# Second layers of two expert stages: two experts to one product of 512 columns

## The reference, cut to what matters

```python
mW1 = W1 + jnp.einsum('be,efh->bfh', g, TW1)
mW2 = W2 + jnp.einsum('be,ehf->bhf', g, TW2)
u = jax.nn.gelu(jnp.einsum('bsh,bfh->bsf', x, mW1) + mb1[:, None, :])
out = jnp.einsum('bsf,bhf->bsh', u, mW2) + mb2[:, None, :]
```

```python
for ei in range(e):
    h = jax.nn.gelu(xf @ W1[ei] + b1[ei], approximate=False)
    y = h @ W2[ei] + b2[ei]
    out = out + y * (gf * mask)[:, None]
```

## Time and profile before

| | |
|---|---|
| median of 3 executions | 468.69 us (468.10 to 469.07) |
| span of the profiled execution | 467.3 us |
| TensorE busy | 449.3 us, 96% |
| VectorE, ScalarE, GpSimd busy | 256.2, 240.2, 123.5 us |
| second layers of stage 1 (L1850, L1830) | about 286.6 to 314.3 us |
| second layers of stage 2 | about 440.0 to 464.5 us |

### The profile page before, as it was taken

How to read it: one execution, slowest core, us unless ns; L and a number is a source line. 1 busy time by engine, 2 the same in 40 slices (tenths; PEclk the granted TensorE clock), 3 DMA queues, 4 the chain that set the end, 5 groups by cost and what they waited for, 6 DMA issues and landing times.

```text
span 467.3 us, 8504 instructions
## 1 busy us (share of the span) xinstructions
PE 449.3 (96%) x3500; PEld 385.6 (83%) x3500; DVE 256.2 (55%) x455; ACT 240.2 (51%) x439; POOL 123.5 (26%) x113
## 2 busy tenths in 40 slices
PE   8999999999999999999987999999999999999997
PEld 7887989989897989899966677998666779778797
DVE  2656223245426232232045788985567765469996
ACT  2577334264445343242113777762788764347872
POOL 1110000002000500000021277966920000019795
PEclk9999999999999999999999999999999999999999
DMA  8925400005200020000039999998000039264000
GB/s 281 412 96 194 180 2 1 1 0 183 89 0 1 13 90 1 1 1 1 1 121 426 362 294 337 420 389 361 2 1 1 2 119 418 96 269 181 0 1 13
DMA packets 13191, 62.65 MB, mean 134 GB/s; under 512 B 1365, under 2 KB 3813, under 8 KB 7392
## 3 DMA queue, kind: packets, MB, share of 16 engines
q1 hardware_dynamic: 11072, 54.31, 30.8%
q0 software_dynamic: 2080, 7.80, 4.7%
HBM read 61.97 MB, written 0.13 MB: 133 GB/s over the span
## 4 chain that ended last, share of the span: by engine, by line
PE 76%; DVE 6%; ACT 5%; DMA 5%; POOL 3%; issue 3%; SPq 0%; DVEq 0%; ACTq 0%; POOLq 0%
PE W L1590 20%; PE W L1546 15%; PE W L1749 7%; PE W L1830 4%; DMA ctxmem<-units_dram 4%; PE W L1884 4%; PE W L1929 3%; PE W L1563 3%; POOL w_lo L552 3%; PE W L1947 2%; PE W L1612 2%; PE W L1469 2%; DMA fixed<-units_dram 1%; PE W L1871 1%; PE W L1498 1%
## 5 line engine op out<-in xcount | busy, mean ns | idle before, releaser
L1590 PE MATMUL W<-probs_turned_hi,ctx_split_hi 128*128 128x256 f32 x256 | 72.8, 285 | 2.6 <-issue 2.5
L1590 PE MATMUL W<-probs_turned_hi,ctx_split_lo 128*128 128x256 f32 x256 | 72.4, 283 | 0.0
L1590 PE MATMUL W<-probs_turned_lo,ctx_split_hi 128*128 128x256 f32 x256 | 72.4, 283 | 0.0
L1024 DVE TENSOR_TENSOR probs_turned_lo<-W,probs_turned_hi 128x512 fp32r<-128x512 f32 x32 | 20.6, 686 | 64.9 <-ACT probs_turned_hi L693 64.9
L1590 PEld LDWEIGHTS W<-probs_turned_hi,ctx_split_hi 128*128 128x128 f32 x256 | 49.1, 192 | 3.8 <-issue 3.3
L561 POOL TENSOR_TENSOR small<-small,const 128x1 f32<-128x1 f32 (+2 forms) x10 | 7.0, 697 | 163.4 <-DVE small L1097 75.3
L1590 PEld LDWEIGHTS W<-probs_turned_lo,ctx_split_hi 128*128 128x128 f32 x256 | 49.1, 192 | 0.2
L1590 PEld LDWEIGHTS W<-probs_turned_hi,ctx_split_lo 128*128 128x128 f32 x256 | 49.1, 192 | 0.0
L712 ACT ACTIVATE pbuf<-W,small 128x1024 f32<-128x1024 f32 x16 | 17.9, 1116 | 59.6 <-DVE small L1044 59.6
L552 POOL TENSOR_TENSOR w_lo<-arena,w_hi 128x320 fp32r<-128x320 f32 x30 | 41.3, 1390 | 26.1 <-ACT w_hi L634 25.6
L552 POOL TENSOR_TENSOR w_lo<-ctxmem,w_hi 128x320 fp32r<-128x320 f32 (+1 forms) x30 | 46.3, 1568 | 5.1 <-ACT w_hi L634 4.6
(11 more groups left out here) (403 smaller groups left out, 907.6 us busy)
## 6 DMA issues: line engine op xcount, KB each, us to landing
arena<-units_dram SPq DMA_DIRECT2D x22, 1024.0 KB, 11.5
ctxmem<-units_dram SPq DMA_DIRECT2D x16, 1024.0 KB, 15.2
fixed<-units_dram SPq DMA_DIRECT2D x6, 1024.0 KB, 6.1
pbuf<-ctx_dram POOLq DMA_DIRECT2D x4, 512.0 KB, 6.3
ctxmem<-ctxT_dram SPq DMA_DIRECT2D x8, 256.0 KB, 11.8
ctxmem<-ctx_dram SPq DMA_DIRECT2D x2, 1024.0 KB, 14.6
scr<-ctx_dram POOLq DMA_DIRECT2D x3, 512.0 KB, 4.2
vecs<-vectors_dram POOLq DMA_DIRECT2D x1, 1040.0 KB, 7.6
```

The source lines that it names most:

```text
L1024: dve.tensor_tensor(PT[1][at], bank(4 + c).rearrange("p (t m) -> p t m", t=4), f32(PT[0][at]), ALU.subtract).then_inc(ev("pl_sb"), 1)
L1590: mm = pe.matmul(ps, CXN[a][:, t, c * P:(c + 1) * P], PT[z][:, t, :], start=(t == 0 and n == 0), stop=(t == KEYT - 1 and n == 2))
```

## The change

Two experts `2m` and `2m + 1` form a pair. A half of a pair holds 2 tiles of both experts instead of 4 tiles of one, laid side by side: the splitting engines read from both units and write the parts with the experts' 256 columns next to each other, so that one product has 512 columns. The third half of a pair is still counted under the second unit, but each half reads both units. For this, `ctxmem` and `arena` become one tensor `memory`, in which both units of a pair are reached with one stride (`memory_of`, `flipped`). There are 24 products of 512 columns for a pair, where there were 48 of 256. `y_ps` counts one sum for a pair, and VectorE adds two experts after it, one behind the other (`add_pair`). The base matrix of stage 1 stays as it was (`base_of_layer2`); the first sum of stage 2 is now that of the pair `m2e0`, `m2e1` (`first_pair_of_layer2`). A unit's place is given free when the pair's last half has been split.

The core of the diff:

```diff
@@ plan_places @@
-            need += lo_done(half_of(before, 1))
+            need += lo_done(half_of(partner(before)[1] if paired(before) else before, 1))
...
-        def half_in(p):
-
-            return unit(SPLIT[p // 2])[:, (p % 2) * HALF:(p % 2 + 1) * HALF]
+        def half_in(p, lo=0, hi=HALF):
+
+            u = SPLIT[p // 2]
+            if paired(u):
+                t = 2 * (p - half_of(partner(u)[0], 0))
+                a, z = sorted(memory_of(v) for v in partner(u))
+                return memory[:, :].rearrange("p (u t c) -> p t u c", u=8 + NA, t=FT)[:, t:t + 2, a:z + 1:z - a, lo // 4:hi // 4]
+            return unit(u)[:, (p % 2) * HALF + lo:(p % 2) * HALF + hi]
...
+        def landed(p):
+
+            u = SPLIT[p // 2]
+            return [(ev(f"place{PLACE[v]}"), LANDED[v]) for v in (partner(u) if paired(u) else (u,))]
...
@@ keep_w_hi @@
-                    act.wait_ge(ev(f"place{PLACE[u]}"), LANDED[u])
+                    for place, count in landed(p):
+                        act.wait_ge(place, count)
...
+            def add_pair(m, n, weight):
+
+                dve.wait_ge(ev("y_ps"), OUTPUTS * n + m + 2)
+                for e in (2 * m, 2 * m + 1):
+                    at = DIM * (e % 2 != flipped(("f2e", "m2e")[n] + str(e)))
+                    dve.scalar_tensor_tensor(out=x[:, :], in0=bank((m + 1) % 4)[:, at:at + DIM], scalar=weight[:, e:e + 1],
+                                             in1=x[:, :], op0=ALU.mult, op1=ALU.add).then_inc(ev("y_used"), 1)
...
+            for m in range(E // 2):
+                keep_w_lo(f"f2e{2 * m + 1}")
+                if m < E // 2 - 1:
+                    keep_w_lo(f"f2e{2 * m + 2}")
+                add_pair(m, 0, gtok)
...
+            def layer2_pair(m, stage):
...
+                def products(p):
+                    first = 4 * (p // 2 - SPLIT.index(("f2e", "m2e")[stage] + str(2 * m))) + 2 * (p % 2)
+                    for t in (first, first + 1):
                         for i, (a, z) in enumerate(TERMS):
+                            mm = pe.matmul(bank((m + 1) % 4), UTS[a][:, t, :],
+                                           w_slot(z, p)[:, (t - first) * 512:(t - first + 1) * 512],
+                                           start=(t == 0 and i == 0), stop=(t == FT - 1 and i == 2))
                     return mm
```

More of the change, by code:

```diff
@@ L65, in half_of, with paired, partner @@
     return 2 * SPLIT.index(u) + n
+def paired(u):
+    return u[1:3] == "2e"
+def partner(u):
+    e = int(u[3:]) // 2 * 2
+    return u[:3] + str(e), u[:3] + str(e + 1)
 def _made_by(maker_of, p):
@@ L107, in lo_done, with ends_output @@
     return [("lo_by_" + maker, sum(1 for q in range(p + 1) if maker in lo_parts(q))) for maker in lo_parts(p)]
+OUTPUTS = 1 + E // 2
+def ends_output(p):
+    u = SPLIT[p // 2]
+    return u[1] == "2" and p % 2 == 1 and (u == "f2b" or int(u[3:]) % 2 == 1)
 def half_used(p):
-    u = SPLIT[p // 2]
-    if u[1] == "2" and p % 2:
-        e = -1 if u == "f2b" else int(u[3:])
-        return "y_ps", e + 2 if u[0] == "f" else E + 2 + e + 1
-    return "w_used", 1 + sum(1 for q in range(p) if not (SPLIT[q // 2][1] == "2" and q % 2))
+    if ends_output(p):
+        u = SPLIT[p // 2]
+        return "y_ps", 1 if u == "f2b" else (2 if u[0] == "f" else OUTPUTS + 2) + int(u[3:]) // 2
+    return "w_used", 1 + sum(1 for q in range(p) if not ends_output(q))
 NR, NA, NB, NC = 4, 5, 3, 4
@@ L210, with memory_of, flipped @@
 LANDED = {unit: 16 * sum(1 for _, q, _ in PLAN[:n + 1] if q == place) for n, (unit, place, _) in enumerate(PLAN)}
+def memory_of(u):
+    n = PLACE[u] - NR
+    return NB + NC + 1 + n if n < NA else (n - NA + NC) % (NB + NC)
+def flipped(u):
+    first, second = partner(u)
+    return memory_of(first) > memory_of(second)
 def bc(ap, axis, n):
@@ L1174, in _ @@
             use_hidden(0, "f2e0")
-            for n in range(E + 1):
-                if n < E:
-                    keep_w_lo(f"f2e{n}", (0, 1) if n else [1])
-                dve.wait_ge(ev("y_ps"), n + 1)
-                if n == 0:
-                    dve.tensor_tensor(x[:, :], bank(0)[:, 0:DIM], x[:, :], ALU.add).then_inc(ev("y_used"), 1)
-                else:
-                    dve.scalar_tensor_tensor(out=x[:, :], in0=bank(n % 4)[:, 0:DIM], scalar=gtok[:, n - 1:n],
-                                             in1=x[:, :], op0=ALU.mult, op1=ALU.add).then_inc(ev("y_used"), 1)
-                dve.wait_ge(ev("y_used"), n + 1)
+            keep_w_lo("f2e0", [1])
+            dve.wait_ge(ev("y_ps"), 1)
+            dve.tensor_tensor(x[:, :], bank(0)[:, 0:DIM], x[:, :], ALU.add).then_inc(ev("y_used"), 1)
+            dve.wait_ge(ev("y_used"), 1)
+            for m in range(E // 2):
[3 more added lines that the diff above has]
+                add_pair(m, 0, gtok)
             give(norm(x[:, :], hn[:, :], 1e-5))
@@ L1851, in products, with first_pair_of_layer2 @@
                                                w_slot(z, p)[:, (t % 4) * DIM:(t % 4 + 1) * DIM],
-                                               start=(u == "m2e0" and t == part == z == 0), stop=(t == FT - 1 and part == 1))
+                                               start=False, stop=(t == FT - 1 and part == 1))
                     return mm
-                return split_products(u, products)
+                return split_products("f2b", products)
+            def first_pair_of_layer2():
+                for hf in range(2):
+                    halves = [half_of(f"m2e{hf}", n) for n in range(2)]
+                    pe.wait_ge(ev("uh_sb"), 2 + hf + 1)
+                    for part in range(2):
+                        if part == 1:
+                            if hf == 0:
+                                turn_hidden(1, 1)
+                            pe.wait_ge(ev("ul_sb"), 2 + hf + 1)
+                        for p in halves:
+                            if part == 0:
+                                for made_by, count in lo_done(p):
+                                    pe.wait_ge(ev(made_by), count)
+                            for n in range(2):
+                                t = 4 * hf + 2 * (p % 2) + n
+                                for z in [z for a, z in TERMS if a == part]:
+                                    mm = pe.matmul(bank(1), UTS[part][:, t, :], w_slot(z, p)[:, n * 512:(n + 1) * 512],
+                                                   start=(t == part == z == 0), stop=(t == FT - 1 and part == 1))
+                            if part == 1 and half_used(p)[0] == "w_used":
+                                mm.then_inc(ev("w_used"), 1)
+                mm.then_inc(ev("y_ps"), 1)
@@ L1856, in _ @@
             pe.matmul(bank(0)[:, 0:DIM], G3T[0:96, :], BR[0:96, F:NROWS], start=True, stop=False)
-            first_of_layer2("f2b", 0).then_inc(ev("y_ps"), 1)
-            for e in range(E):
-                layer2(f"f2e{e}", e + 1).then_inc(ev("y_ps"), 1)
+            base_of_layer2().then_inc(ev("y_ps"), 1)
+            for m in range(E // 2):
+                layer2_pair(m, 0)
             stay_warm(5, 11)
@@ L2162, in _ @@
                 .then_inc(ev("y_ps"), 1)
-            first_of_layer2("m2e0", E + 2).then_inc(ev("y_ps"), 1)
-            for e in range(1, E):
-                layer2(f"m2e{e}", E + 2 + e).then_inc(ev("y_ps"), 1)
+            first_pair_of_layer2()
+            for m in range(1, E // 2):
+                layer2_pair(m, 1)
 def _unit(*parts):
```

65 lines of the change are left out of this document (33 added, 32 removed).

## The result

The changed kernel takes 478.71 us (median of 4 runs, 476.48 to 479.81) where the kernel before takes 468.88 us beside it: ratio 1.0195, 95% interval 1.0158 to 1.0231. Slower was forecast, but 473.6 us and at most 476.5 us. The profiled execution of after is one of 478.5 us, with a span of 476.7 us, 9.4 us above that of before.

A forecast was written before the change was run, and what follows sets the result against it. Splitting engines were taken to pace both second layers behind TensorE's high share; span 467.3 + 3.5 (stage 1) + 1.4 (stage 2) = 472.2 us, median 1.4 us above, so 473.6 us; range 470.6 to 476.5 us.

The forecast's parts named there:

- the cover of `f2e0`'s lone split: Stage 1: `f2e0` used to be split and multiplied while `f2e1` was still on its way; pairing loses this.
- Stage 1's start: First cast waits for `f2e1`, so VectorE begins the pair's third-half low parts at 294.5 instead of 291.59, 2.9 us late.
- Stage 2's turn: Eight wide products precede the turn of the hidden values' second half, so VectorE's low parts start 0.9 us late.
- Splitting in runs at nothing: Both stages: reading and writing the split parts in 4 runs was taken to cost nothing; upper end some 17 us.
- rival C: Runs cost 0.18 us on each of 26 paced halves, +4.7 us, giving 478.3 us; chance 0.11.
- Products at nothing: TensorE: 192 wide products are 2.1 us less work than 384 narrow, but nearly all stays idle time.
- rival B: TensorE becomes the bound in the steady part, a pair takes 5.58 us, -2.3 us, giving 471.3 us; chance 0.16.
- From then on VectorE has 4 low parts and 2 adds per pair: Stage 1's steady part: VectorE's work per pair was put at 6.1 us, as before, so no cost was added.
- at the end one more add, 0.5 us: End of each stage: two adds stand behind the last product where one stood, 0.5 us more.
- So `f2e1` is there at about 290.4 us: Stage 1: `f2e1`'s landing read from ScalarE's DMA wait, 3.6 us after `f2e0`'s first half was cast.
- rival D: TensorE's clock falls while standing still between the base matrix's halves, +1.4 us, giving 475.0 us; chance 0.13.
- The forecast's 0.5 us for `f2e3`: Stage 1's next pair: `f2e3` cast to 297.5 us while VectorE would be ready at 297.0 us, 0.5 us more.

The follow-up runs named there:

- 28 warm products: Changed kernel with 28 products of constants on TensorE ahead of the base matrix's second half in stage 1; 478.32 us, ratio 1.0184.
- the run that was mended: Changed kernel with context loads five behind `f2e1`, five behind `f2e7`, a pair's adds taken apart, stage 2's turn earlier; 469.92 us, ratio 1.0002.
- Stage 1 alone: Changed kernel with pairs only in stage 1, stage 2 as before the change; 476.80 us, ratio 1.0135.
- The repeat of after: The changed kernel run once more without any edit; 478.21 us, ratio 1.0171.
- the first two: Changed kernel with all ten context loads behind `f2e1`, 477.93 us, 1.0170; with five behind `f2e1`, five behind `f2e3`, 476.97 us, 1.0157.

## Why the prediction was right in kind and too small

**Right.** Slower, by the loss of the cover of `f2e0`'s lone split, and by the turn. Stage 1's start: the row of low parts behind the base's add was forecast 2.9 us late. From the activation it begins after 10.36 us (286.36 to 296.72) instead of 7.05 (284.54 to 291.59), 3.3 us late. That this is close to 2.9 is in part luck: from the cast on it took 4.63 us where 4.1 were forecast, since the clock had fallen (3.86 with 28 warm products), and `f2e1` landed 0.2 us earlier than forecast. Stage 2's turn: 0.9 forecast, 0.91 by the run that undoes it. Splitting in runs at nothing: VectorE's low part, when it runs alone, takes 0.89 us in both kernels, the means of the halves are 1328 and 1319 ns (VectorE, GpSimd) against 1331 to 1344 and 1390 to 1447 before, and in the run that was mended the low parts keep the 2.55 us for two of the earlier trace rows; rival C is out. Products at nothing: TensorE waits for low parts; rival B did not come, since the period of a pair grew.

**The step that failed, first:** "From then on VectorE has 4 low parts and 2 adds per pair, 4 x 1.27 + 2 x 0.5 = 6.1 us, as before", and with it "at the end one more add, 0.5 us". In after the four low parts take 5.13 to 5.37 us, a pair 6.07 to 6.33 us. Before, two experts take 5.95 us (2 x 2.98), so the sum of 6.1 was itself not "as before", and it was charged nowhere. While the adds stand together, TensorE waits for the next low parts; then the last two low parts lie 1.1 us apart (2.17 for both) and not 1.3, and TensorE, which needs 1.40 us for each, ends 2.33 us behind them instead of 1.86. The forecast had 0.5 us a stage for the end and nothing for the rest; the runs give 1.06 and 0.88 us for the lump alone, on top of the extra add.

**Second:** "So `f2e1` is there at about 290.4 us" was taken from one trace as if it were a time of the program. It was 5.9 us after the activation there; over the seven profiles with paired units in stage 1 and the loads' old order it was 5.7, 5.7, 6.7, 8.1, 8.9, 9.0 and 9.4 us. Now such a lateness is all on the path: stage 1 took 35.0 us at 5.7 and 38.6 us at 9.0 and 9.4. Before, TensorE had 24 narrow products of `f2e0` to do meanwhile, 2.9 us; whether they would cover a late landing is argued and not shown, since the two unpaired profiles with this order of loads have it at 5.8 and 5.9 us. Stage 1 alone costs 1.35%, 6.3 us, and not the 4.7 of the profile with an early landing, which fits. Part of the lateness is in the transfers before: from 265 to 290 us, with the DMA engines busy all the time, the queue moved 316 to 320 GB/s in the profiles with 5.7 and 5.8 us and a stage that starts at about 286.3 us, and 309, 304 and 292 in those with 6.7, 8.1 and 8.9 us. Those 28 GB/s over 25 us are 1.7 us at 415 GB/s, half of the 3.2. The repeat of after and the run with 28 warm products:

```profile
265.00:290.00 25.00, 24.47 (x111) 18.64 (x109) 19.52 (x23) 18.17 (x27) 16.38 (x12) 1.00 1.04 320
265.00:290.00 25.00, 24.46 (x109) 18.60 (x108) 19.79 (x24) 18.17 (x27) 16.36 (x12) 1.00 1.03 292
```

No instruction of a pair has run by then, so the pairs are not its cause. Why the rate differs, and where the other half comes from, was not found out.

**Third:** rival D, the clock at the base's matrix, was not a rival but came with the forecast's own wait. It came in each profile with a wait there except that of 28 warm products. It was priced at 1.4 us and cost 0.6 to 1.9 us. The forecast's 0.5 us for `f2e3` did not show in after, since TensorE was later still.

**Sum.** Forecast 4.9 us over the span: 3.5 and 1.4. Found in the same trace: 4.7 and 2.5, 0.4 between, and 1.8 us of falls of the clock in unchanged code. The stages close with the terms found: 3.3 for the late start, 0.9 for the lump and 0.5 for the last add in stage 1; 0.9 for the turn, 1.1 and 0.5 in stage 2. The 2.2 us outside the stages were chance of this execution and no term of a forecast; by the runs of one stage each the change costs 6.3 and 2.2 us, where 3.5 and 1.4 were forecast.

## What to carry to other kernels

If one product is made to need two transfers, it waits for the later one: before pairing, read not only when each lands but what else stands in the queue between them, and move the loads that are needed last behind those that are needed next. Do it in one go up to the end of the stage: each half measure here moved the wait to a later pair, and the first two gained nothing that shows (ratios 1.0170 and 1.0157, against 1.0171). When two consumers are served by one engine, taking work in lumps costs even if its sum is the same. And a wider product saves nothing where its operands' producers set the pace: mended in every point found, the pairs only came back to no change.
